# Two full-tile additions of an adaLN block made by accumulating DMAs instead of by GpSimd

## The chip, the cores and the metric

One NeuronCore of a Trainium2 chip runs the whole program, a transformer block over 8 batch rows of 2048 tokens with 256 features, all float32. The metric is the device time of one execution in microseconds (us), lower is better.

## The reference, cut to what matters

```python
h = layernorm(x) * (1 + ca) + sa
a = attention(h)            # per head: softmax over the 64x64 matrix q^T k, then v times it, then w_fc, + b_fc + h
a = layernorm(a) * gamma + beta
x2 = x + ga * a             # = x + (ga*gamma) * norm(..) + ga*beta
h2 = layernorm(x2) * (1 + cb) + sb
y = gb * sigmoid(r(h2)) * (relu(k(h2))**2 @ W_v)    # r and k mix each token with the one before it
out = x2 + y
```

`ga`, `gb`, `ca` and the like are vectors of 256 numbers, one set for each batch row.

## The kernel before, in words

Tokens lie on the 128 partitions. A batch row `b` is cut into four chunks `j` of 512 tokens; a chunk is a tile of 128 partitions by 1024 numbers (four token groups `t` of 256 features), 512 KB. Each engine has its instruction order written out by hand (`row_steps` of each engine), and rows 1 to 5 or 6 run in a hardware loop. The orders interleave three rows: the second half of row `b`, the statistics, transposes and score matrix of row `b+1`, and the loads and statistics of row `b+2`. All joints are semaphores.

The way of one chunk through the second half: TensorE multiplies (`attention`); ScalarE squares (`squares`, L625); GpSimd makes the factor `rs_o` (`rstd_o`, L452 and L454); VectorE scales the product (`make_x2`, L874) and adds `xb` (L881), which gives `x2`; VectorE takes statistics (`stats_2`, L887); GpSimd makes the normalisation factors (`rstd_2`, eleven instructions on 128x4 numbers, L425 to L447); ScalarE normalises (`make_z2`, L679); TensorE transposes; ScalarE copies; VectorE mixes with the token before (`mix`, L901 and L905); then the three products of the second part, with `split_xr` (L642), `low_xr` (L912), `take_r` (L651, writes the gate into `y`), `low_k` (L919) and `gate_o` (L928, makes `y`).

Two additions on whole tiles are GpSimd's: `make_xb` (L462) makes `xb = x_in + ga*beta` for the next row, and `add_y` (L480) makes `y = y + x2`, which SyncE then stores (`store_y`). GpSimd's order in a loop row is `rstd_o(b,0)`, `add_y(b-1,2)`, `rstd_2(b,0)`, `prep_wv` (L469 to L475), `rstd_o(b,1)`, `make_xb(n,0)`, `rstd_2(b,1)`, `make_xb(n,1)`, `rstd_o(b,2)`, `add_y(b-1,3)`, `rstd_2(b,2)`, `make_xb(n,2)`, `rstd_o(b,3)`, `add_y(b,0)`, `make_xb(n,3)`, `rstd_2(b,3)`, two `rstd_a`, `add_y(b,1)`, two `rstd_a`, where `n = b+1`. Before the loop GpSimd makes the four `xb` of row 0. SyncE issues the loads of `x_in` (L294; each waits until `z` and `xb` have been made from the old data), the loads of broadcast rows from a scratch in memory, and the stores. `y` has two buffers by turns; `take_r` waits until the store from its buffer has ended (`y_stored`). In the last row ("alone") the `x_in` buffers serve as more `y` buffers, and `make_x2` waits there until `add_y` of the row before has read the `x2` chunk that it overwrites.

Of the kernel before, what the change touches and what calls it, by code (L numbers as in the profile page):

```python
# [26 lines left out]
ALU = mybir.AluOpType  # L27
# [3 lines left out]
P = 128  # L31


def adaln_block(nc, x, w_qkv, b_qkv, w_fc, b_fc, gamma, beta, w_r, w_k, w_v, mu_r, mu_k, c, wmod, out):
    B, L, D = x.shape
# [6 lines left out]
    CH = L // CT  # L42
    NT = CT // P
# [10 lines left out]
    with ExitStack() as ctx:  # L54
# [9 lines left out]
        def sem(name):  # L64
            return ctx.enter_context(nc.semaphore(name))
# [91 lines left out]
        def y_buf(j, alone):  # L157

            return x_in[:, j] if alone else y[:, j % 2]
# [86 lines left out]
        z_ready = sem("z_ready")  # L246
        z_turned = sem("z_turned")
        z_used = sem("z_used")
        z_t_ready = sem("z_t_ready")
        xb_ready = sem("xb_ready")  # L250
        att_done = sem("att_done")
        ssq_ready = sem("ssq_ready")
        ve_o_done = sem("ve_o_done")
# [21 lines left out]
        th_ready = sem("th_ready")  # L275
        o_done = sem("o_done")
        ro_ready = sem("ro_ready")
        y_ready = sem("y_ready")
        y_end_stored = sem("y_end_stored")
        y_end_ready = sem("y_end_ready")  # L280
        y_stored = [sem(f"y_stored{s}") for s in range(2)]
# [1 line left out]
        def wait_past(eng, semaphore, count):  # L283

            if not isinstance(count, int) or count > 0:
                eng.wait_ge(semaphore, count)
# [4 lines left out]
        @block.sync  # L291
        def _(sp):
            def load_x(b, j):
                sp.dma_start(x_in[:, j], x_v[b, j]).then_inc(x_loaded[j], 16)  # L294

            def load_ca(b):
                src = scratch[b, CA:CA + D].partition_broadcast(P)
                sp.dma_start(rows[:, 3], src).then_inc(ca_loaded, 16)

                sp.dma_start(wqk_aug[P - 1:P, KD - 1, :], scratch[b, QB:QB + QK].unsqueeze(0)).then_inc(edge_loaded, 16)  # L300
                sp.dma_start(res[P - 1:P, KD - 1, :], scratch[b, CB:CB + D].unsqueeze(0)).then_inc(edge_loaded, 16)

            def load_gates(b):

                src = scratch[b, GB:GB + 2 * D].partition_broadcast(P)
                sp.dma_start(rows[:, 0:2].rearrange("p r d -> p (r d)"), src).then_inc(gates_loaded, 16)

            def load_gb(b):
                src = scratch[b, GB + 2 * D:NR].partition_broadcast(P)
                sp.dma_start(rows[:, 2], src).then_inc(gb_loaded, 16)  # L310

            def next_x(b, j):

                sp.wait_ge(z_ready, CH * (b - 1) + j + 1)
                sp.wait_ge(xb_ready, CH * (b - 1) + j + 1)
                load_x(b, j)

            def next_ca(b):

                sp.wait_ge(m_ready, b)  # L320
                sp.wait_ge(wv_ready, b)
                load_ca(b)

            def next_gates(b):

                sp.wait_ge(xb_ready, CH * b)
                sp.wait_ge(now_step, 3 * b - 2)
                load_gates(b)

            def next_gb(b):  # L330

                sp.wait_ge(now_ready, b)
                load_gb(b)

            def store_y(b, j, alone=False):
                sp.wait_ge(y_ready, CH * b + j + 1)
                sp.dma_start(out_v[b, j], y_buf(j, alone)).then_inc(y_stored[j % 2], 16)

            def row_steps(b, first):
                next_gates(b + 1)  # L340
                if not first:
                    store_y(b - 1, 2)
                next_x(b + 2, 0)
                next_x(b + 2, 1)
                if not first:
                    store_y(b - 1, 3)
                next_gb(b + 1)
                next_x(b + 2, 2)
                next_x(b + 2, 3)
                store_y(b, 0)  # L350
                store_y(b, 1)
                next_ca(b + 2)

            wmod_v = wmod.rearrange("(k p) n -> p k n", p=P)
            sp.dma_start(c_sb, c).then_inc(c_loaded, 16)
            load_x(0, 0)
            sp.dma_start(wmod_sb[:, :, 0:2 * D], wmod_v[:, :, 0:2 * D]).then_inc(wmod_a_loaded, 16)
            load_x(0, 1)
            load_x(0, 2)
            sp.dma_start(wmod_sb[:, :, 2 * D:6 * D], wmod_v[:, :, 2 * D:6 * D]).then_inc(wmod_b_loaded, 16)  # L360
            load_x(0, 3)
            for n, w in enumerate((w_r, w_k, w_v)):
                sp.dma_start(w_ffn[:, n], w.rearrange("(k p) n -> p k n", p=P)).then_inc(ffn_loaded, 16)

            sp.wait_ge(row8_a_ready, 1)
            sp.dma_start(scratch[:, 0:GB], row8[:, 0:GB]).then_inc(row8_stored, 16)
            sp.wait_ge(row8_stored, 16)
            load_ca(0)
            sp.wait_ge(row8_b_ready, 1)
            sp.dma_start(scratch[:, GB:NR], row8[:, GB:NR]).then_inc(row8_stored, 16)  # L370
            sp.wait_ge(row8_stored, 32)
            load_gates(0)
            load_gb(0)
            for j in range(CH):
                next_x(1, j)
            next_ca(1)
            row_steps(0, True)
            with sp.Fori(1, B - 2) as b:
                row_steps(b, False)
            next_gates(B - 1)  # L380
            store_y(B - 3, 2)
            store_y(B - 3, 3)
            next_gb(B - 1)
            for b in (B - 2, B - 1):
                for j in range(CH):
                    if b < B - 1 or j < CH - 1:
                        store_y(b, j, alone=(b == B - 1 and j > 0))

            for q in range(2):
                half = slice(2 * q, 2 * q + 2)  # L390
                sp.wait_ge(y_end_ready, q + 1)
                sp.dma_start(out_v[B - 1, CH - 1, :, half], y_buf(CH - 1, True)[:, half]).then_inc(y_end_stored, 16)

            sp.wait_ge(y_stored[0], 16 * B * CH // 2)
            sp.wait_ge(y_stored[1], 16 * (B * CH // 2 - 1))
            sp.wait_ge(y_end_stored, 32)
# [3 lines left out]
        def _(pool):  # L400
# [52 lines left out]
                pool.wait_ge(ve_o_done, i + 1)  # L453
                nc.gpsimd.tensor_tensor(rs_o[:, s], ve_o[:, s], neg_half[:], ALU.pow).then_inc(rs_o_ready, 1)  # L454

            def make_xb(b, j, first=False):
                pool.wait_ge(x_loaded[j], 16 * (b + 1))
                pool.wait_ge(gates_loaded, 16 * (b + 1))
                if not first:

                    pool.wait_ge(x2_ready, CH * (b - 1) + j + 1)
                nc.gpsimd.tensor_tensor(xb[:, j], x_in[:, j], rows[:, 1].unsqueeze(1).to_broadcast([P, NT, D]),  # L462
                                        ALU.add).then_inc(xb_ready, 1)

            def prep_wv(b):

# [8 lines left out]
                nc.gpsimd.tensor_copy(wv_aug[:, :, LAST], vb_col[:, :, b]).then_inc(wv_ready, 1)  # L475

            def add_y(b, j, alone=False):
                i, y_j = CH * b + j, y_buf(j, alone)
                pool.wait_ge(ro_ready, 2 * i + 2)
                nc.gpsimd.tensor_tensor(y_j, y_j, x2[:, j], ALU.add).then_inc(y_ready, 1)  # L480

            def row_steps(b, first, far):

# [58 lines left out]
            pool.wait_ge(vb_ready, 1)  # L542
            prep_wv(0)
            for j in range(CH):
                make_xb(0, j, first=True)
            rstd_a(1, 0)
            rstd_a(1, 1)
            row_steps(0, True, True)
# [7 lines left out]
        def _(act):  # L556
# [56 lines left out]
            def squares(b, j, alone=False):  # L613


                i, s = CH * b + j, j % 2
                if alone:
                    act.wait_ge(xb_ready, i + 1)
                elif j == CH - 1:
                    wait_past(act, y_ready, CH * b)  # L620
                sq_out = x_in if alone else x2
                for t in range(NT):
                    if t % 2 == 0:
                        act.wait_ge(att_done, 2 * i + t // 2 + 1)
                    sq = nc.scalar.activation(sq_out[:, j, t], att_banks(j, alone)[t // 2][:, (t % 2) * D:(t % 2 + 1) * D], ACT.Square,  # L625
                                              scale=float(D) ** -0.5, accum_out=ssq[:, s, t:t + 1])
                sq.then_inc(ssq_ready, 1)
# [150 lines left out]
        def _(dve):  # L778
# [89 lines left out]
            def make_x2(b, j, mixes=None, alone=False):  # L868

                i, s = CH * b + j, j % 2  # L870
                wait_past(dve, xk_mixed, CH * b + (max(j - 1, 0) if mixes is None else mixes))
                dve.wait_ge(rs_o_ready, i + 1)
                for t in range(NT):
                    ins = nc.vector.scalar_tensor_tensor(t_buf[:, t], att_banks(j, alone)[t // 2][:, (t % 2) * D:(t % 2 + 1) * D],  # L874
                                                         rs_o[:, s, t:t + 1], g_row[:], ALU.mult, ALU.mult)
                ins.then_inc(t_done, 1)
                dve.wait_ge(t_done, i + 1)
                dve.wait_ge(xb_ready, i + 1)
                if alone:
                    dve.wait_ge(y_ready, CH * (b - 1) + j + 1)  # L880
                nc.vector.tensor_tensor(x2[:, j], t_buf[:], xb[:, j], ALU.add).then_inc(x2_ready, 1)  # L881

            def stats_2(b, j):
# [595 lines left out]
```

## Time and profile before

| | |
|---|---|
| time, median of 3 runs | 775.9 us (775.25 to 776.17) |
| the profiled execution | 776.98 us; its span 775.2 us |
| mean granted TensorE clock in it | 0.971 |
| stores of `y` / loads of `x_in`, 512 KB each | 31 whole ones and two halves / 32 |
| issue to landing, median | 3.0 us / 3.5 us |
| DMA queues' share of 16 engines | 16.3% (SyncE's queue), 1.0% (ScalarE's) |
| one loop row (GpSimd's L469 at 173.1, 262.1, 352.5, 442.9, 531.8 us) | 89.0 to 90.4 us |

The span runs from the first to the last instruction; the 1.8 us between it and the execution's time lie around the program. A timeline row gives start and duration of an instruction (or of some in a row, x2, x4), and in brackets how long its engine had been idle and what released it. The trace names the `x2` tile `x`.

### The profile page before, as it was taken

The numbers are of one execution on the slowest core, as the hardware profiler recorded it, in microseconds if no ns is written. First come the engines' busy times: TensorE is split into PE (matmuls) and PEld (weight loads), VectorE is DVE, ScalarE is ACT, GpSimd is POOL, SyncE is SP. The second block draws the span as 40 slices with busy tenths as digits, with TensorE's granted clock in tenths as the row PEclk, the third lists the DMA queues.
The fourth block names the chain that finished last, engine by engine and source line by source line (L and its number), as shares of the span: only waits on it lengthen the run. The fifth ranks groups of instructions, "written<-read, shape, count | busy, mean of one in ns | idle before, by whom it ended". The sixth has DMA issues, their size and how long they took to land.

```text
span 775.2 us, 11980 instructions
## 1 busy us (share of the span) xinstructions
PE 679.2 (88%) x3810; PEld 545.9 (70%) x3810; DVE 626.0 (81%) x1063; ACT 422.8 (55%) x903; POOL 497.3 (64%) x809
## 2 busy tenths in 40 slices
PE   5958888998889888998889989898889988898687
PEld 1847776886768775877768867687758777687565
DVE  4595879968998699886999589986998879857864
ACT  0323563565655466455745656554754557456654
POOL 4155897588656785768755886558856687407542
PEclk8989988999999999999999999999999999999999
DMA  9213021111211122010210112120221101100002
GB/s 314 66 52 100 1 89 54 35 42 48 69 55 48 54 61 81 28 48 27 88 54 34 41 54 61 54 70 31 61 81 33 42 0 34 39 16 28 28 27 82
DMA packets 40810, 43.22 MB, mean 56 GB/s; under 512 B 2697, under 2 KB 38833, under 8 KB 40785
## 3 DMA queue, kind: packets, MB, share of 16 engines
q1 hardware_dynamic: 38704, 40.24, 16.3%
q10 hardware_dynamic: 2080, 2.68, 1.0%
q8 instruction: 12, 0.20, 0.1%
q14 instruction: 14, 0.11, 0.0%
HBM read 26.06 MB, written 16.85 MB: 55 GB/s over the span
## 4 chain that ended last, share of the span: by engine, by line
POOL 40%; DVE 19%; issue 18%; PE 17%; DMA 2%; ACT 2%; POOLq 1%; DVEq 0%; ACTq 0%
POOL xb L462 5%; DVE x L881 3%; POOL ag L437 3%; POOL y L480 3%; POOL rs_o L454 3%; POOL ag_a L437 3%; DVE xk L905 3%; DVE t_buf L874 3%; POOL ag L425 2%; POOL ag L431 2%; PE work L1308 2%; POOL wv_aug L469 2%; POOL ag L427 2%; POOL ag_a L431 2%; DVE st L887 2%
## 5 line engine op out<-in xcount | busy, mean ns | idle before, releaser
L1258 PE MATMUL att<-m_sb,z_t 128*128 128x256 f32 x496 | 113.3, 381 | 17.3 <-DVE t_buf L874 16.3
L679 ACT ACTIVATE z<-x,ag 128x256 f32<-128x256 f32 x128 | 66.4, 590 | 100.5 <-POOL ag L447 100.5
L1258 PEld LDWEIGHTS att<-m_sb,z_t 128*128 128x128 f32 x496 | 92.3, 190 | 35.1 <-issue 23.9
L874 DVE SCALAR_TENSOR_TENSOR t_buf<-att,rs_o,g_row 128x256 f32<-128x256 f32 x124 | 51.4, 478 | 68.7 <-POOL rs_o L454 68.6
L1308 PE MATMUL work<-xk,w_k_t 128*128 128x512 f32 x236 | 106.2, 592 | 0.0
L1142 PE MATMUL work<-wvf_lo,k_hi 128*128 128x256 f32 x248 | 75.8, 306 | 28.3 <-issue 23.8
L462 POOL TENSOR_TENSOR xb<-x_in,rows 128x1024 f32<-128x1024 f32 x32 | 79.3, 2482 | 16.0 <-DMA rows<-row_scratch 8.5
L1240 PE MATMUL gram<-z 128*128 128x256 f32 (+1 forms) x512 | 89.1, 327 | 0.0
L425 POOL TENSOR_TENSOR ag<-st 128x4 f32<-128x4 f32 x32 | 20.6, 643 | 102.4 <-DVE st L887 102.4
L1240 PEld LDWEIGHTS gram<-z 128*128 128x128 f32 x512 | 79.8, 191 | 6.6
L1142 PE MATMUL work<-w_r_lo,xr_hi 128*128 128x256 f32 x232 | 69.1, 298 | 11.6 <-DVE xr_lo L912 11.6
L1142 PEld LDWEIGHTS work<-wvf_lo,k_hi 128*128 128x128 f32 x248 | 49.9, 201 | 41.2 <-issue 34.1
L480 POOL TENSOR_TENSOR y<-y,x 128x1024 f32<-128x1024 f32 x29 | 68.8, 2373 | 9.8 <-DVE y L928 9.8
L1308 PEld LDWEIGHTS work<-xk,w_k_t 128*128 128x128 f32 x236 | 42.8, 190 | 42.6 <-issue 42.6
L642 ACT ACTIVATE xr_hi<-xr 128x1024 fp32r<-128x1024 f32 x30 | 31.6, 1054 | 75.3 <-DVE xr L905 75.2
L1144 PE MATMUL work<-wvf_hi,k_lo 128*128 128x256 f32 x248 | 72.7, 293 | 0.0
L1143 PE MATMUL work<-wvf_hi,k_hi 128*128 128x256 f32 x248 | 72.6, 293 | 0.0
L1143 PE MATMUL work<-w_r_hi,xr_hi 128*128 128x256 f32 x232 | 66.3, 286 | 0.0
L1144 PE MATMUL work<-w_r_hi,xr_lo 128*128 128x256 f32 x232 | 66.2, 285 | 0.0
L864 DVE TENSOR_SCALAR z<-x_in,ag_a 128x255 f32<-128x255 f32 x128 | 56.2, 501 | 7.7 <-PE gram L1240 3.9
L625 ACT ACTIVATE x<-att 128x256 f32<-128x256 f32 x116 | 42.9, 379 | 23.9 <-PE att L1258 23.8
L881 DVE TENSOR_TENSOR x<-t_buf,xb 128x1024 f32<-128x1024 f32 x32 | 52.1, 1629 | 4.1 <-POOL y L480 3.0
(187 smaller groups left out, 1780.1 us busy)
## 6 DMA issues: line engine op xcount, KB each, us to landing
x_in<-in_L_attn_x_dram SPq DMA_DIRECT2D x32, 512.0 KB, 3.5
out_dram<-y SPq DMA_DIRECT2D x29, 512.0 KB, 3.0
rows<-row_scratch SPq DMA_DIRECT2D x16, 128.0 KB, 3.5
rows<-row_scratch SPq DMA_DIRECT2D x8, 256.0 KB, 3.2
wqkv_sb<-in_L_attn_w_qkv_dram ACTq DMA_DIRECT2D x1, 1536.0 KB, 10.7
x<-in_L_wmod_dram SPq DMA_DIRECT2D x1, 1024.0 KB, 14.0
out_dram<-x_in SPq DMA_DIRECT2D x2, 512.0 KB, 3.0
x<-in_L_wmod_dram SPq DMA_DIRECT2D x1, 512.0 KB, 4.6
```

Of the source, the lines that this page charges most:

```text
L462: nc.gpsimd.tensor_tensor(xb[:, j], x_in[:, j], rows[:, 1].unsqueeze(1).to_broadcast([P, NT, D]), ALU.add).then_inc(xb_ready, 1)
L480: nc.gpsimd.tensor_tensor(y_j, y_j, x2[:, j], ALU.add).then_inc(y_ready, 1)
L679: ins = nc.scalar.activation(z2[:, t], x2[:, j, t], ACT.Identity, bias=ag_2[:, s, 1, t:t + 1], scale=ag_2[:, s, 7, t:t + 1])
L864: ins = nc.vector.tensor_scalar(z[:, j % 2, t, 0:LAST], x_in[:, j, t, 0:LAST], ag_a[:, j, 3, t:t + 1], ag_a[:, j, 7, t:t + 1], ALU.subtrac ...
L874: ins = nc.vector.scalar_tensor_tensor(t_buf[:, t], att_banks(j, alone)[t // 2][:, (t % 2) * D:(t % 2 + 1) * D], rs_o[:, s, t:t + 1], g_ro ...
L881: nc.vector.tensor_tensor(x2[:, j], t_buf[:], xb[:, j], ALU.add).then_inc(x2_ready, 1)
L1142: mm(dst, s_hi, m_lo, start=start, stop=False)
L1143: mm(dst, s_hi, m_hi, start=False, stop=False)
L1144: return mm(dst, s_lo, m_hi, start=False, stop=stop)
L1240: ins = mm(gram[:, k * D:(k + 1) * D - k * P], z[:, j % 2, t, k * P:(k + 1) * P], z[:, j % 2, t, k * P:D], start=(j == 0 and t == 0 and k ...
L1258: ins = mm(att_banks(j, alone)[q][:, (t % 2) * D:(t % 2 + 1) * D], z_t[:, j, k, t * P:(t + 1) * P], m_sb[:, k], start=(k == 0), stop=(k == ...
L1308: ins = mm(k_banks(alone)[dh][:], w_k_t[:, ch, rows_dh], mixed(j, alone)[1][:, ch], start=(ch == 0), stop=(ch == KD - 1))
```

## The change: what it does

`make_xb` and `add_y` are DMAs issued by GpSimd that add in flight. For `x2 + y`, SyncE stores `x2` to the output as soon as it is made, and GpSimd's DMA adds `y` to it in memory. For `x + ga*beta`, SyncE fills the `xb` chunk with the broadcast row (as soon as `x2` of the old row is made), and GpSimd's DMA adds `x`, read again from memory, to it. The waits follow: the loads of `x_in` and of the gates no longer wait for `xb`; `squares` waits for the store of the old `x2` chunk; `make_x2` waits for the DMA into its `xb` chunk. The order of GpSimd's steps stays as it is; SyncE's order is new.

```diff
             def load_gates(b):
-                src = scratch[b, GB:GB + 2 * D].partition_broadcast(P)
-                sp.dma_start(rows[:, 0:2].rearrange("p r d -> p (r d)"), src).then_inc(gates_loaded, 16)
+                src = scratch[b, GB:GB + D].partition_broadcast(P)
+                sp.dma_start(rows[:, 0], src).then_inc(gates_loaded, 16)
+            def fill_xb(b, j):
+                src = scratch[b, GB + D:GB + 2 * D].partition_broadcast(P).unsqueeze(1).to_broadcast([P, NT, D])
+                sp.dma_start(xb[:, j], src).then_inc(xb_filled[j], 16)
...
-            def store_y(b, j, alone=False):
-                sp.wait_ge(y_ready, CH * b + j + 1)
-                sp.dma_start(out_v[b, j], y_buf(j, alone)).then_inc(y_stored[j % 2], 16)
+            def store_x2(b, j):
+                sp.wait_ge(x2_ready, CH * b + j + 1)
+                sp.dma_start(out_v[b, j], x2[:, j]).then_inc(x2_stored[j], 16)
+            def store_and_fill(b, j):
+                store_x2(b, j)
+                fill_xb(b + 1, j)
+            def row_steps(b):
                 next_gates(b + 1)
                 next_x(b + 2, 0)
                 next_x(b + 2, 1)
+                store_and_fill(b, 0)
+                next_x(b + 2, 2)
+                store_and_fill(b, 1)
                 next_gb(b + 1)
+                store_and_fill(b, 2)
                 next_x(b + 2, 3)
+                store_and_fill(b, 3)
                 next_ca(b + 2)
...
             load_gb(0)
             for j in range(CH):
+                fill_xb(0, j)
+            for j in range(CH):
                 next_x(1, j)
...
+            def make_xb(b, j):
+                pool.wait_ge(xb_filled[j], 16 * (b + 1))
+                nc.gpsimd.dma_start(xb[:, j], x_v[b, j], accum_op=ALU.add).then_inc(xb_ready[j], 16)
...
             def add_y(b, j, alone=False):
                 pool.wait_ge(ro_ready, 2 * i + 2)
-                nc.gpsimd.tensor_tensor(y_j, y_j, x2[:, j], ALU.add).then_inc(y_ready, 1)
+                pool.wait_ge(x2_stored[j], 16 * (b + 1))
+                nc.gpsimd.dma_start(out_v[b, j], y_buf(j, alone), accum_op=ALU.add).then_inc(y_stored[j % 2], 16)
...
-                dve.wait_ge(xb_ready, i + 1)
+                dve.wait_ge(xb_ready[j], 16 * (b + 1))
                 if alone:
-                    dve.wait_ge(y_ready, CH * (b - 1) + j + 1)
+                    dve.wait_ge(x2_stored[j], 16 * b)
```

## Rows read from the trace of the kernel before

**Rows 1.** The page, part 1: busy time of each engine over the span.

```profile
PE 679.2 (88%) x3810; PEld 545.9 (70%) x3810; DVE 626.0 (81%) x1063; ACT 422.8 (55%) x903; POOL 497.3 (64%) x809
```

**Rows 2.** The page, part 4: the chain that ended last, shares by engine.

```profile
POOL 40%; DVE 19%; issue 18%; PE 17%; DMA 2%; ACT 2%; POOLq 1%; DVEq 0%; ACTq 0%
```

**Rows 3.** Busy us by stretch, one loop row: length, engines, TensorE clock, DMA.

```profile
262.00:352.00 90.00, 81.61 (x463) 66.35 (x462) 77.35 (x128) 51.84 (x112) 61.69 (x100) 0.98 0.17 53
```

**Rows 4.** VectorE waiting for others, same row (us in total, times, longest).

```profile
DVE t_buf L874 <- POOL rs_o L454: 10.0, 3, 6.3
```

**Rows 5.** Groups of instructions, GpSimd (busy us, mean ns, idle before).

```profile
L462 POOL TENSOR_TENSOR xb<-x_in,rows 128x1024 f32<-128x1024 f32 x32 | 79.3, 2482 | 16.0 <-DMA rows<-row_scratch 8.5 <-DVE x L881 7.5
L480 POOL TENSOR_TENSOR y<-y,x 128x1024 f32<-128x1024 f32 x29 | 68.8, 2373 | 9.8 <-DVE y L928 9.8
```

**Rows 6.** Timeline of GpSimd in that row: start, duration, instruction, idle before.

```profile
277.72 2.37 POOL L462 TENSOR_TENSOR xb<-x_in,rows 128x1024 f32<-128x1024 f32 x1
291.05 2.88 POOL L462 TENSOR_TENSOR xb<-x_in,rows 128x1024 f32<-128x1024 f32 x1
294.62 1.40 POOL L454 TENSOR_TENSOR rs_o<-ve_o,neg_half 128x4 f32<-128x4 f32 x1
297.65 2.39 POOL L480 TENSOR_TENSOR y<-y,x 128x1024 f32<-128x1024 f32 x1 [1.63 <-DVE y L928]
301.30 2.35 POOL L462 TENSOR_TENSOR xb<-x_in,rows 128x1024 f32<-128x1024 f32 x1 [1.25 <-DVE x L881]
310.10 0.21 POOL L425 TENSOR_TENSOR ag<-st 128x4 f32<-128x4 f32 x1 [6.45 <-DVE st L887]
```

**Rows 7.** Timeline of VectorE in that row.

```profile
277.74 2.89 DVE L953 TENSOR_TENSOR wvf_lo<-t_buf,wvf_hi 128x512 fp32r<-128x512 f32 x1
281.82 1.66 DVE L874 SCALAR_TENSOR_TENSOR t_buf<-att,rs_o,g_row 128x256 f32<-128x256 f32 x4 [1.19 <-POOL rs_o L454]
297.49 1.66 DVE L874 SCALAR_TENSOR_TENSOR t_buf<-att,rs_o,g_row 128x256 f32<-128x256 f32 x4
299.18 1.95 DVE L881 TENSOR_TENSOR x<-t_buf,xb 128x1024 f32<-128x1024 f32 x1
301.35 3.38 DVE L901 TENSOR_TENSOR t_buf<-h2t 128x1024 f32<-128x1024 f32 x1 [0.22 <-PE work L1308]
```

**Rows 8.** By source line, ns min/median/max, then first and last start.

```profile
L881 DVE TENSOR_TENSOR x<-t_buf,xb x32: 1224/1678/1961, 73.9 to 731.0; 128x1024 f32<-128x1024 f32 x32
...
L901 DVE TENSOR_TENSOR t_buf<-h2t x32: 1206/1216/3383, 86.7 to 750.9; 128x1024 f32<-128x1024 f32 x32
...
L431 POOL TENSOR_SCALAR ag<-ag x32: 192/193/1728, 77.6 to 740.0; 128x4 f32<-128x4 f32 x32
```

**Rows 9.** Timeline of ScalarE in that row.

```profile
294.07 1.05 ACT L642 ACTIVATE xr_hi<-xr 128x1024 fp32r<-128x1024 f32 x1
317.37 1.31 ACT L651 ACTIVATE y<-work 128x512 f32<-128x512 f32 x2
```

**Rows 10.** Timeline of TensorE around 309 us.

```profile
308.81 0.36 PE L1142 MATMUL work<-wvf_lo,k_hi 128*128 128x256 f32 x1 [2.40 <-issue]
310.97 0.41 PE L1142 MATMUL work<-wvf_lo,k_hi 128*128 128x256 f32 x1
```

**Rows 11.** By tile, x_in: SyncE's issues (ns), and issue to landing (us).

```profile
L294 SPq DMA_DIRECT2D x_in<-in_L_attn_x_dram x32: 368/373/518, 1.2 to 573.6; - x32
DMA to landing us min/median/max: 2.6/3.5/15.1
```

**Rows 12.** Timeline of SyncE at the start, its slowest issue.

```profile
5.45 5.75 SPq L363 DMA_DIRECT2D y<-in_L_ffn_W_k_dram  x1
```

**Rows 13.** Timeline of VectorE: start, first row, last row.

```profile
52.13 4.76 DVE L1002 TENSOR_TENSOR attn<-s_exp,s_inv 64x256 f32<-64x256 f32 x2
121.11 5.63 DVE L905 SCALAR_TENSOR_TENSOR xr<-t_buf,mu_col,h2t 128x512 f32<-128x512 f32 x2
...
730.99 1.23 DVE L881 TENSOR_TENSOR x<-t_buf,xb 128x1024 f32<-128x1024 f32 x1 [3.00 <-POOL y L480]
```

More of the change, by code:

```diff
@@ L249, in adaln_block @@
         z_t_ready = sem("z_t_ready")
-        xb_ready = sem("xb_ready")
+        xb_filled = [sem(f"xb_filled{j}") for j in range(CH)]
+        xb_ready = [sem(f"xb_ready{j}") for j in range(CH)]
         att_done = sem("att_done")
@@ L277, in adaln_block @@
         ro_ready = sem("ro_ready")
-        y_ready = sem("y_ready")
+        x2_stored = [sem(f"x2_stored{j}") for j in range(CH)]
         y_end_stored = sem("y_end_stored")
@@ L314, in next_x @@
                 sp.wait_ge(z_ready, CH * (b - 1) + j + 1)
-                sp.wait_ge(xb_ready, CH * (b - 1) + j + 1)
                 load_x(b, j)
@@ L324, in next_gates @@
             def next_gates(b):
-                sp.wait_ge(xb_ready, CH * b)
                 sp.wait_ge(now_step, 3 * b - 2)
@@ L333, in next_gb @@
                 load_gb(b)
-            def store_y(b, j, alone=False):
-                sp.wait_ge(y_ready, CH * b + j + 1)
-                sp.dma_start(out_v[b, j], y_buf(j, alone)).then_inc(y_stored[j % 2], 16)
-            def row_steps(b, first):
+            def store_x2(b, j):
[5 more added lines that the diff above has]
+            def row_steps(b):
                 next_gates(b + 1)
-                if not first:
-                    store_y(b - 1, 2)
                 next_x(b + 2, 0)
                 next_x(b + 2, 1)
-                if not first:
-                    store_y(b - 1, 3)
+                store_and_fill(b, 0)
+                next_x(b + 2, 2)
+                store_and_fill(b, 1)
                 next_gb(b + 1)
-                next_x(b + 2, 2)
+                store_and_fill(b, 2)
                 next_x(b + 2, 3)
-                store_y(b, 0)
-                store_y(b, 1)
+                store_and_fill(b, 3)
                 next_ca(b + 2)
@@ L374, in _ @@
             for j in range(CH):
+                fill_xb(0, j)
+            for j in range(CH):
                 next_x(1, j)
             next_ca(1)
-            row_steps(0, True)
+            row_steps(0)
             with sp.Fori(1, B - 2) as b:
-                row_steps(b, False)
+                row_steps(b)
             next_gates(B - 1)
-            store_y(B - 3, 2)
-            store_y(B - 3, 3)
+            store_and_fill(B - 2, 0)
+            store_and_fill(B - 2, 1)
             next_gb(B - 1)
[L384 to L387, printed above, removed]
+            store_and_fill(B - 2, 2)
+            store_and_fill(B - 2, 3)
+            for j in range(CH - 1):
+                store_x2(B - 1, j)
             for q in range(2):
@@ L454, in rstd_o @@
                 nc.gpsimd.tensor_tensor(rs_o[:, s], ve_o[:, s], neg_half[:], ALU.pow).then_inc(rs_o_ready, 1)
[L456 to L463, printed above, removed]
+            def make_xb(b, j):
+                pool.wait_ge(xb_filled[j], 16 * (b + 1))
+                nc.gpsimd.dma_start(xb[:, j], x_v[b, j], accum_op=ALU.add).then_inc(xb_ready[j], 16)
             def prep_wv(b):
@@ L477, in add_y @@
             def add_y(b, j, alone=False):
-                i, y_j = CH * b + j, y_buf(j, alone)
+                i = CH * b + j
                 pool.wait_ge(ro_ready, 2 * i + 2)
-                nc.gpsimd.tensor_tensor(y_j, y_j, x2[:, j], ALU.add).then_inc(y_ready, 1)
+                pool.wait_ge(x2_stored[j], 16 * (b + 1))
+                nc.gpsimd.dma_start(out_v[b, j], y_buf(j, alone), accum_op=ALU.add).then_inc(y_stored[j % 2], 16)
             def row_steps(b, first, far):
@@ L544, in _ @@
             for j in range(CH):
-                make_xb(0, j, first=True)
+                make_xb(0, j)
             rstd_a(1, 0)
@@ L617, in squares @@
                 if alone:
-                    act.wait_ge(xb_ready, i + 1)
-                elif j == CH - 1:
-                    wait_past(act, y_ready, CH * b)
+                    act.wait_ge(z_ready, i + 1)
+                else:
+                    wait_past(act, x2_stored[j], 16 * b)
                 sq_out = x_in if alone else x2
```

## The prediction, made before the changed kernel ran

> **What bounds the kernel now.** The page's busy shares come first [rows 1]: TensorE 88%, VectorE 81%, GpSimd 64%. No engine is full, so a wait or the order of work sets the pace. The chain that ended last says which [rows 2]: GpSimd holds 40% of it, VectorE 19%, TensorE 17%. The engine with a middling busy share is on the path most. Next one loop row by itself [rows 3]: of 90.0 us TensorE is busy 81.6, VectorE 77.4, GpSimd 61.7, the DMA engines 0.17. The first number is the floor: a row cannot fall much below 81 us whatever GpSimd does, so at most some 8.4 us a row are to be had. The waits of the same row [rows 4]: VectorE stands 10.0 us in three places, each time for `rs_o`, the small factor that GpSimd makes. GpSimd's groups [rows 5] give the two additions that leave it: 32 of 2.48 us and 29 of 2.37 us (and two in the last row).
>
> The timelines show two ways in which a whole-tile addition hurts. First by order: in the second chunk GpSimd ends its normalisation factors at 277.7, then spends 2.37 us on `xb`, and only then makes the `rs_o` for which VectorE is idle 1.19 us [rows 6, 7]. Second by slowing VectorE: while such an addition runs, VectorE's own additions of two tiles take longer. L881 takes 1.22 us at best, 1.68 at the median, 1.96 at most; L901 1.21 at the median and 3.38 at 301.35, exactly beside the `xb` of 301.30 [rows 6 to 8].
>
> **The change, part by part, for one loop row.** The new quantity is T, the time for which GpSimd is held by issuing one adding DMA; the trace has none. From below stands SyncE's issue of a plain 512 KB DMA, 0.37 us [rows 11]; from above SyncE's slowest issue, 5.75 us [rows 12], and a tile pass of GpSimd is 2.37 to 2.48 us [rows 5]. I take T = 2.0: nearer to the tile pass than to the issue of SyncE, since 512 pieces of 1 KB have to be described for two sides. Then eight times a row 2.4 us become 2.0, which is little; the gain lies in where the rest goes.
>
> 1. *The addition `x2` no longer meets a GpSimd pass.* Chunks 0, 1 and 2 go from the median 1.68 to 1.22, the fourth from 1.95 to 1.22 [rows 7, 8]: 3 x 0.45 + 0.7 = 2.05 us. All four stand before the statistics that GpSimd waits for, so they count in full.
> 2. *`rs_o` of the third chunk comes earlier by 2.37 - T = 0.4 us.* VectorE could use it: the 2.89 us of L953 from 277.74 [rows 7] were themselves stretched by the `xb` beside them, and become less than the 4.1 us until L874.
> 3. *L901 of the third mix, 3.38 to 1.21: 2.2 us.* VectorE has no gap from 297.49 to there [rows 7], and what comes behind it is `low_k` and the statistics of the fourth chunk.
> 4. *TensorE's gap before `ffn_out`, 2.40 us, closes*, because it waits for that `low_k` [rows 10]. Behind the gap the matmuls slow down: one at 310.97 takes 0.41 us, the first took 0.36 [rows 10]. Over the whole row the granted clock is 0.98, which on 81.6 busy us is some 1.6 us [rows 3]. The gap itself closes by items 1 to 3 and is not counted again; of the 1.6 I take 1.0 (bounds 0 and 1.6).
> 5. *The stretched second mix (L905) is worth nothing.* It lies beside ScalarE's copy of `xr`, which begins at 294.07 [rows 9] and on which the next VectorE step waits; that copy hangs on GpSimd's factors. The cover is about 2 us.
> 6. *What the new waits cost.* The fill of chunk j starts when `x2` of that chunk is made and SyncE has issued the store: 2 x 0.37 us, then 3.5 us as a load of the same size [rows 11], and 1.4 us more since the store goes ahead of it on the same queue (my estimate, some 40% of a landing). So a fill is there 5.6 us after `x2`. GpSimd stands at `make_xb` until then, with all that is queued behind it. For chunk 0 the DMA is due 12 us later or more. For chunk 2, `x2` is ready about 285 and the `xb` step is at 291.05: just enough. `rs_o` behind it ends at 296.0 and is used at 297.49 [rows 6, 7], so T may grow to 2.88 + 1.5 = 4.4 us there. For chunk 3 it is late: in the clock of the old trace `x2` ends at 300.4, the fill lands at 306.0, GpSimd is free at 308.0, and the statistics it should take up are ready at 310.1 [rows 6] less 0.7 and 2.2, that is 307.2. Cost 0.8 us, of which I count 0.6 because the exponentials behind it have a little slack.
> 7. *Landing of the adding DMAs.* `xb` for chunk 3 has most of a row until its use. `y` of chunk 0 is issued at 297.65 and its buffer is written again at 317.37 [rows 6, 9]: 19.7 us of cover for something whose plain relatives take 3.5 at the median and 15.1 at most [rows 11]. Nothing counted. The DMA share rises from 0.17 [rows 3]: two transfers of 512 KB a chunk become five, with two of them reading twice, so about 0.17 x 7 / 2 = 0.6. That fits.
>
> SyncE's moved steps: `next_x` loses its wait for `xb` and comes earlier; the stores of `x2` wait for VectorE only, and no step behind them is due before. `next_gates` and `next_gb` keep waits that end early in the row. Nothing counted.
>
> Sum: 2.05 + 0.4 + 2.2 + 1.0 - 0.6 = 5.05 us a row. With six such rows (1 to 6) 30 us. TensorE's floor allows it: 5.05 of 8.4.
>
> *Row 0*: the pair of L905 at 121.11 takes 5.63 where two plain ones take 1.5 [rows 13]: 4 us. *Last row*: VectorE's wait of 3.00 us for `add_y` turns into a wait for a store long ended [rows 13]: 3 us. *Start*: the addition beside `attn` made that 4.76 instead of about 0.85 us [rows 13], a gain of 3.9. Against it four fills go ahead of the loads of row 1 on SyncE's queue, up to 4 x 3.5 = 14 us if they don't overlap, and the statistics of those loads stand in VectorE's order before the matrix that starts row 0. I set the two equal: 0, bounds +4 and -10. *End*: the last whole chunk went 2.37 + 3.0 us by addition and store, now T + 3.5 to 7 us by one DMA: 1 us lost (0 to 4).
>
> Total 30 + 4 + 3 + 0 - 1 = 36. The profiled execution is 776.98 us, so 741; it stands 1.1 us above the median of 775.9, so I predict **740 us**. With T = 0.4 item 2 gives 1.6 more and item 6 falls away, 2.2 a row: about 727. With T = 4, the row keeps 5.05 - 2 x 2.0 = 1.05 (each us of T counts in items 2 and 6): 764.
>
> L881 and L901 are slowed beside a tile pass of GpSimd [rows 6 to 8]. The Trainium skill (SBUF — State Buffer, section "Who interferes with whom") says that a VectorE instruction with two inputs in SBUF contends with a GpSimd instruction that reads SBUF, and the page infers that building descriptors needs the write side, which such an instruction leaves free. The trace agrees with the first half; no row here shows the second. By it T stays at its undisturbed value and items 1 and 3 come in full. The same page, section "SBUF: two separate sides", speaks against the change: a DMA of GpSimd has its descriptors written by software, and one that takes 0.62 us alone took 3.1 us beside a VectorE copy. An estimate by that 3.1: 5.05 - 2.2 = 2.85 us a row, 754 us in all; rival A works out the same kind of hindrance from rows.
>
> **Rivals.**
>
> *A, GpSimd's issue and VectorE still hinder each other (0.15).* For it: a 128x4 step of GpSimd takes 0.19 us and up to 1.73 [rows 8] when VectorE is in the way, so each issue may be held 1.5 us, T = 3.5. Against: GpSimd no longer streams tiles. The row keeps 5.05 - 3.0 = 2.05; 6 x 2.05 + 4 + 3 - 1 = 18, so 759 us.
>
> *B, slower: the issue of an adding DMA holds GpSimd longer than the addition did (0.20).* Each stands in GpSimd's order before small factors that the other engines wait for. Items 2 and 6 lose T - 2 each; zero is reached at T = 2 + 5.05 / 2 = 4.5 us. At the upper bound 5.75 they cost 7.5, and the `rs_o` of chunk 3 (allowed 4.4) another 1.35: 3.8 us lost a row, 27 over seven, and the last row's 3 back, 4 lost at the end: 805 us. For it: one plain issue did take 5.75 [rows 12]. Against: the 32 loads of `x_in` took 0.37 to 0.52 to issue [rows 11].
>
> *C, slower: the fill lands late (0.07).* GpSimd stands at `make_xb` and all factors behind it wait. At the 15.1 us that one load took [rows 11], `make_xb` of chunk 2 ends about 303 and its `rs_o` 304.9, 7.4 us after VectorE wants it; with the gains left some 7 to 8 us are lost a row, 830 us. Against: that load was one of the start's crowd.
>
> *D, a tie (0.06)*: T near 4.5, or adding DMAs that land after the 19.7 us of item 7, give back just the gain: 776 us. That the additions don't leave GpSimd at all is excluded, since they are no longer its instructions.
>
> **How the numbers follow.** The forecast, with its own range 720 to 768, has 0.52. A and the forecast are faster: 0.67. The tie, and measurements of this kernel can't tell 0.2% (1.6 us) from no change, has 0.06. B and C are slower: 0.27. The range 718 to 800 leaves out the upper part of B, C, and a little below.
>
> **What would show it.** GpSimd's busy time should fall by the 148 us of [rows 5] (issuing a DMA isn't counted as busy), L881 be near 1.22 us in all chunks, L901 never above 1.3, VectorE's wait for `rs_o` below 10 us a row, a row about 85 us. SyncE's and GpSimd's waits tell item 6: a wait of GpSimd for the fills above 2 us a row means C; small factors that follow an issue by more than 3 us mean B. Most likely to be wrong is T, then the start.

## The result, and the profile after

The changed kernel takes **819.5 us** at the median (814.4 to 823.5, 4 runs), beside 775.6 us for the kernel before on the same chip: ratio 1.058 [1.050, 1.065]. It is slower, outside the range; the prediction said 740 us. The execution shown here took 817.35 us, its span is 815.8 us.

The page of the changed kernel, parts 1, 3 and 4, and one group of part 5 (busy us and mean ns; idle time before it, and what ended it):

```profile
span 815.8 us, 12092 instructions
...
PE 688.3 (84%) x3810; PEld 549.3 (67%) x3810; DVE 556.4 (68%) x1063; ACT 421.0 (52%) x903; POOL 407.5 (50%) x809
...
q1 hardware_dynamic: 55600, 55.97, 28.4%
q0 software_dynamic: 33264, 33.03, 27.3%
...
DMA 31%; POOL 25%; issue 15%; DVE 13%; PE 10%; ACT 2%; SPq 2%; POOLq 1%; DVEq 0%; ACTq 0%
...
L466 POOL DMA_DIRECT2D xb<-in_L_attn_x_dram x32 | 42.6, 1331 | 165.5 <-DMA xb<-row_scratch 165.5
```

Against [rows 1], VectorE has 70 us and GpSimd 90 us less to do: both reliefs came. Yet every engine is idle longer. The chain says why: DMA holds 31% of it and held 2% before [rows 2]. The last line names the transfer. GpSimd stands 165.5 us at the adding DMA of `make_xb` (L466), waiting for the fill of `xb` from `row_scratch`.

Part 6 of the page: KB of each DMA, median us from issue to landing.

```profile
x_in<-in_L_attn_x_dram SPq DMA_DIRECT2D x32, 512.0 KB, 5.9
xb<-row_scratch SPq DMA_DIRECT2D x32, 512.0 KB, 9.9
xb<-in_L_attn_x_dram POOLq DMA_DIRECT2D x32, 512.0 KB, 5.9
out_dram<-x SPq DMA_DIRECT2D x31, 512.0 KB, 4.4
out_dram<-y POOLq DMA_DIRECT2D x29, 512.0 KB, 6.1
```

The adding DMAs land in 5.9 and 6.1 us. The slow one is the plain fill: 9.9 us, where the prediction worked with 3.5 for the same bytes, and 1.4 more for the store ahead.

The chain of waits, one loop row (start us, us, what). It answers to [rows 2] at the scale of a row:

```profile
288.91 1.02 POOL rs_o L461
...
290.35 1.27 DVE t_buf L878 x3
291.65 1.24 DVE x L885
293.17 0.40 SPq L340
293.67 9.70 DMA xb<-row_scratch
...
304.04 1.34 POOL xb L466
305.38 0.24 POOL ve_o L459
305.71 1.03 POOL rs_o L461
...
307.17 1.27 DVE t_buf L878 x3
308.46 1.24 DVE x L885
309.85 0.40 SPq L340
310.33 10.12 DMA xb<-row_scratch
```

It is a loop through four parties: `rs_o` lets VectorE make `x2` of a chunk, SyncE stores it and fills `xb` of that chunk, the fill lets GpSimd issue `make_xb`, and behind that in GpSimd's order stands the `rs_o` of the next chunk. One turn is 16.8 us, 10 of them the fill. GpSimd's timeline shows the same from its side (start, duration, idle before); it answers to [rows 6]:

```profile
304.03 1.35 POOL L466 DMA_DIRECT2D xb<-in_L_attn_x_dram  x1 [2.38 <-DMA xb<-row_scratch]
305.70 1.03 POOL L461 TENSOR_TENSOR rs_o<-ve_o,neg_half 128x4 f32<-128x4 f32 x1
306.70 1.32 POOL L484 DMA_DIRECT2D out_dram<-y  x1
...
321.08 1.34 POOL L466 DMA_DIRECT2D xb<-in_L_attn_x_dram  x1 [5.50 <-DMA xb<-row_scratch]
322.74 1.03 POOL L461 TENSOR_TENSOR rs_o<-ve_o,neg_half 128x4 f32<-128x4 f32 x1
...
338.54 1.28 POOL L466 DMA_DIRECT2D xb<-in_L_attn_x_dram  x1 [13.49 <-DMA xb<-row_scratch]
339.32 0.74 POOL L432 TENSOR_TENSOR ag<-st 128x4 f32<-128x4 f32 x1
```

Three chunks wait for their fills, 21.4 us in this row. The issue itself holds GpSimd for 1.3 us.

*Where the 40.6 us of span come from.* The starts of `prep_wv` (L469 before, L472 after) mark the rows, the first `x2` the end of the start. (The five times that the table of the kernel before gives for L469 are those of its L472, 2.5 us later; the row lengths there hold.)

| stretch (us) | before | after | difference |
|---|---|---|---|
| span's start to first `x2` addition | 73.85 | 98.33 | +24.5 |
| to `prep_wv` of the first loop row | 96.8 | 91.6 | -5.1 |
| five loop rows | 449.1 | 467.7 | +18.6 |
| from there to the end | 155.5 | 158.1 | +2.6 |

A row is 93.5 us instead of 89.8. So there are two losses, the start and the row, and both were to be explained. VectorE's timeline at the start, answering to [rows 13]:

```profile
51.23 0.85 DVE L1006 TENSOR_TENSOR attn<-s_exp,s_inv 64x256 f32<-64x256 f32 x2
...
81.50 1.40 DVE L858 BATCH_NORM_STATS2 st_a<-x_in 128x6 f32<-128x256 f32 x4 [28.70 <-DMA x_in<-in_L_attn_x_dram]
```

`attn` is short, as forecast, but the statistics behind it wait 28.7 us for the loads that stand behind four fills on SyncE's queue. What TensorE and the DMA engines do meanwhile (columns as in [rows 3], the last two DMA share and GB/s):

```profile
60.00:66.00 6.00, 0.29 (x2) 0.00 (x0) 0.00 (x0) 0.00 (x0) 1.30 (x1) 0.70 0.87 83
```

The DMA engines are 87% busy and move only 83 GB/s. GpSimd's issues of `make_xb` follow the fills at 56.8, 63.6, 70.0 and 77.4 us: 6.4 to 7.4 us for each fill of 512 KB. Little else moves meanwhile, though it has been issued: the adding DMA of 56.8 lands 24.3 us later.

### The profile page after: what moved, and what is told of

It reads as the page before. It is cut to its first block, busy times and chain, and to the rows that moved or that the text cites. A ratio compares the mean times of both kernels' runs of the same rounds, so it can differ in the third digit from the quotient of the medians.

```text
span 815.8 us, 12092 instructions
## 1 busy us (share of the span) xinstructions
PE 688.3 (84%) x3810; PEld 549.3 (67%) x3810; DVE 556.4 (68%) x1063; ACT 421.0 (52%) x903; POOL 407.5 (50%) x809
## 4 chain that ended last, share of the span: by engine, by line
DMA 31%; POOL 25%; issue 15%; DVE 13%; PE 10%; ACT 2%; SPq 2%; POOLq 1%; DVEq 0%; ACTq 0%
DMA xb<-row_scratch 26%; DVE t_buf L878 4%; DMA x_in<-in_L_attn_x_dram 4%; DVE x L885 4%; POOL rs_o L461 3%; POOL xb L466 2%; POOL ag L444 2%; PE att L1262 2%; POOL ag L432 2%; PE work L1312 1%; POOL out_dram L484 1%; POOL ag_a L438 1%; POOL wv_aug L472 1%; DMA wqkv_sb<-in_L_attn_w_qkv_dram 1%; POOL wv_aug L475 1%
## 5 line engine op out<-in xcount | busy, mean ns | idle before, releaser
L1262 PE MATMUL att<-m_sb,z_t 128*128 128x256 f32 x496 | 115.7, 387 | 47.7 <-DVE m_sb L1013 27.9
L1262 PEld LDWEIGHTS att<-m_sb,z_t 128*128 128x128 f32 x496 | 94.0, 193 | 66.3 <-issue 54.3
L1312 PE MATMUL work<-xk,w_k_t 128*128 128x512 f32 x236 | 115.9, 631 | 22.1 <-ACT y L655 22.1
L466 POOL DMA_DIRECT2D xb<-in_L_attn_x_dram x32 | 42.6, 1331 | 165.5 <-DMA xb<-row_scratch 165.5
L1148 PE MATMUL work<-wvf_hi,k_lo 128*128 128x256 f32 x248 | 71.0, 286 | 0.0
L1147 PE MATMUL work<-wvf_hi,k_hi 128*128 128x256 f32 x248 | 70.9, 286 | 0.0
L858 DVE BATCH_NORM_STATS2 st_a<-x_in 128x6 f32<-128x256 f32 x128 | 44.5, 409 | 34.5 <-DMA x_in<-in_L_attn_x_dram 34.3
L432 POOL TENSOR_TENSOR ag<-st 128x4 f32<-128x4 f32 x32 | 23.2, 725 | 71.1 <-DVE st L891 71.1
L1146 PEld LDWEIGHTS work<-w_r_lo,xr_hi 128*128 128x128 f32 x232 | 44.4, 191 | 11.6 <-DVE xr_lo L916 11.6
L868 DVE TENSOR_SCALAR z<-x_in,ag_a 128x255 f32<-128x255 f32 x128 | 45.8, 419 | 9.4 <-POOL ag_a L444 5.3
```

The lines of the kernel that those rows point to most:

```text
L466: nc.gpsimd.dma_start(xb[:, j], x_v[b, j], accum_op=ALU.add).then_inc(xb_ready[j], 16)
L858: ins = nc.vector.bn_stats(st_a[:, j, t], x_in[:, j, t])
L868: ins = nc.vector.tensor_scalar(z[:, j % 2, t, 0:LAST], x_in[:, j, t, 0:LAST], ag_a[:, j, 3, t:t + 1], ag_a[:, j, 7, t:t + 1], ALU.subtrac ...
L1146: mm(dst, s_hi, m_lo, start=start, stop=False)
L1147: mm(dst, s_hi, m_hi, start=False, stop=False)
L1148: return mm(dst, s_lo, m_hi, start=False, stop=stop)
```

## The experiments

Each was timed in three rounds beside the kernel before (775.85 us in the first four, 775.32 in the rest). The ratio is to that kernel. Diffs are against the changed kernel unless said, and show the main lines; `...` marks what is left out. The length of a row is the mean of the five loop rows of the profiled execution.

Theory one, *the source of the fill*: all 512 pieces of a fill read the same 1 KB row, and that makes it slow. Theory two, *the traffic*: five transfers a chunk share the DMA engines, and a fill is slow because much is in flight or the store is ahead of it. Theory three, *GpSimd and VectorE still hinder each other* (rival A), or the issue is long (B).

**e1: the same pieces, another source.**

```diff
-                src = scratch[b, GB + D:GB + 2 * D].partition_broadcast(P).unsqueeze(1).to_broadcast([P, NT, D])
-                sp.dma_start(xb[:, j], src).then_inc(xb_filled[j], 16)
+                sp.dma_start(xb[:, j], x_v[b, j]).then_inc(xb_filled[j], 16)
```

> The kernel after, but the fill of xb reads 512 different rows of x (the chunk itself) instead of one row of ga*beta 512 times; so xb is 2x, not x + ga*beta. Same 512 KB, same 1 KB pieces, same order and waits. Theory S (one source row read by every piece is slow): a fill lands in 4.5 to 6 us instead of 9.9, GpSimd's wait for fills falls from 165 to under 40 us, the start loses some 5 us instead of 24, and the time is 735 to 765 us. Rival Q (the DMA queues are too full, or 1 KB pieces beside adding DMAs are slow): a fill still lands in 9 to 10 us and the time stays 810 to 825.

Measured: 736.1 us, ratio 0.950 [0.947, 0.954]. Its page, part 6:

```profile
xb<-in_L_attn_x_dram SPq DMA_DIRECT2D x32, 512.0 KB, 6.0
xb<-in_L_attn_x_dram POOLq DMA_DIRECT2D x32, 512.0 KB, 6.1
```

Number, size and target of the pieces, their place in the queue and all traffic are as in the changed kernel; only the addresses read differ. The fill lands in 6.0 us instead of 9.9, a row takes 84.1 us, and 83 us are gone. Theory two cannot say this. One expectation was missed: GpSimd still waits 82.8 us in all for fills (165.5 before the edit), where under 40 were expected. In a loop row it waits 10.4 to 10.8 us, and the row is no longer than in e5 and e8 below, where it waits for no fill: there is slack for this much.

**e2: only the half of `y`**, against the kernel before: `xb` stays an addition of GpSimd.

```diff
+            def store_x2(b, j):
+                sp.wait_ge(x2_ready, CH * b + j + 1)
+                sp.dma_start(out_v[b, j], x2[:, j]).then_inc(x2_stored[j], 16)
...
-                nc.gpsimd.tensor_tensor(y_j, y_j, x2[:, j], ALU.add).then_inc(y_ready, 1)
+                pool.wait_ge(x2_stored[j], 16 * (b + 1))
+                nc.gpsimd.dma_start(out_v[b, j], y_buf(j, alone), accum_op=ALU.add).then_inc(y_stored[j % 2], 16)
...
```

> Only the half that concerns y: x2 is stored, y is added in memory by GpSimd's DMA; xb is made on GpSimd as before, with no fills. Theory W (all that was lost was lost waiting for fills): this half is a gain by itself, since GpSimd is held 1.33 us instead of 2.4 and VectorE is slowed less: 755 to 765 us. Rival (adding DMAs into memory cost time of their own, at the end or by their traffic): 776 or more.

Measured: 760.6 us, 0.981 [0.976, 0.985]; a row 87.2 us. This half gains 15 us; the changed kernel, which has the `xb` half on top, is 59 us slower than this one. So the loss comes with `xb`. VectorE is busy 603.7 us, between 626.0 and 556.4: each half takes away part of the slowing. Part 3 of the page (packets, MB, share of the 16 DMA engines' time) prices the adding DMAs, which alone are on q0 here:

```profile
q1 hardware_dynamic: 38704, 40.24, 16.3%
q0 software_dynamic: 16368, 16.25, 15.6%
```

They keep the DMA engines busy 2.4 times as long for a byte as the plain ones do (0.96% for a MB against 0.41).

**e3: the fill ahead of the store.**

```diff
-                store_x2(b, j)
+                sp.wait_ge(x2_ready, CH * b + j + 1)
                 fill_xb(b + 1, j)
+                store_x2(b, j)
```

> The kernel after, with the fill issued ahead of the store of x2 on SyncE instead of behind it. At the start, with no store ahead, four fills took about 6.6 us each. Theory S with queueing behind the store as the second part: a fill lands in about 7 us instead of 9.9, GpSimd waits some 50 to 70 us less in all and the time falls to 795 to 805 us; the start keeps its 24 us. If the store had no part in it: 9 to 10 us and 815 to 820.

Measured: 788.9 us, 1.018 [1.014, 1.021]; a row 88.5 us. Part 6 of its page:

```profile
xb<-row_scratch SPq DMA_DIRECT2D x32, 512.0 KB, 8.9
xb<-in_L_attn_x_dram POOLq DMA_DIRECT2D x32, 512.0 KB, 6.0
out_dram<-x SPq DMA_DIRECT2D x31, 512.0 KB, 9.7
```

The landing was expected at 7 us and is 8.9: the store costs the fill 1.0 us, less than the 1.4 of the prediction, and the fill is slow even when it is first. The store now pays for standing behind it, 9.7 instead of 4.4 us. The time fell by 31 us, more than the 1.0 us of median landing explains at sight; one turn of the loop above also loses the store's issue (0.4 us), and the wait of GpSimd fell by 27 us. The expected 795 to 805 us was missed, on the fast side; how much each gives was not taken apart.

**e4: the row is loaded once, the fill copies it from on-chip memory.**

```diff
-                src = scratch[b, GB:GB + D].partition_broadcast(P)
-                sp.dma_start(rows[:, 0], src).then_inc(gates_loaded, 16)
+                src = scratch[b, GB:GB + 2 * D].partition_broadcast(P)
+                sp.dma_start(rows[:, 0:2].rearrange("p r d -> p (r d)"), src).then_inc(gates_loaded, 16)
...
-                src = scratch[b, GB + D:GB + 2 * D].partition_broadcast(P).unsqueeze(1).to_broadcast([P, NT, D])
+                sp.wait_ge(gates_loaded, 16 * (b + 1))
+                src = rows[:, 1].unsqueeze(1).to_broadcast([P, NT, D])
...
             def next_gates(b):
+                for j in range(CH):
+                    sp.wait_ge(xb_filled[j], 16 * b)
```

> The kernel after, but the row of ga*beta is loaded once per batch row into the rows tile (128 KB, as before the change) and the fill copies it from there inside on-chip memory, each partition its own row. Nothing is left out. Theory S: no row in memory is read by all pieces, so a fill lands in 4 to 6 us and the time is 735 to 765 us. Rival Q: 9 to 10 us, 810 to 825 us.

Measured: 743.6 us, 0.959 [0.955, 0.963]; the full computation. Part 6:

```profile
xb<-rows SPq DMA_DIRECT2D x32, 512.0 KB, 5.9
```

Each piece now reads the copy of its own partition (four pieces share it), and the fill lands in 5.9 us. A row takes 84.1 us, as in e1. The 7.5 us above e1 lie in the start: the first `x2` comes at 83.8 instead of 75.6 us. Waiting for the load of the row explains part of it: the four fills are issued 2.8 us later than in e1 (51.04 instead of 48.27). The first statistics of row 1's load then begin 7.6 us later (67.74 instead of 60.16); where the rest comes from was not found.

**e5: the same slow fills, but `make_xb` later in GpSimd's order.**

```diff
                     rstd_o(b, 1)
-                    make_xb(n, 0)
                     rstd_2(b, 1)
-                    make_xb(n, 1)
                     rstd_o(b, 2)
                     add_y(b - 1, 3)
+                    make_xb(n, 0)
                 rstd_2(b, 2)
...
-                make_xb(n, 2)
                 rstd_o(b, 3)
...
+                make_xb(n, 1)
                 add_y(b, 0)
-                make_xb(n, 3)
                 rstd_2(b, 3)
...
                 add_y(b, 1)
+                make_xb(n, 2)
...
+                make_xb(n, 3)
```

> The kernel after with the fill as it is (slow, one row of memory), but GpSimd issues the adding DMAs of xb later in its order, where the fills have long landed: chunk 0 behind add_y(b-1,3), chunk 1 behind rstd_o(b,3), chunk 2 behind add_y(b,1), chunk 3 at the row's end. Theory: it is GpSimd standing in a wait, with the small factors behind it, that costs the rows, not the traffic; then the waits for fills in the loop vanish, only the start's (some 31 us on GpSimd, 24 us in the time) stay, and the time is 755 to 770 us. Rival: slow fills and adding DMAs disturb the rows by traffic: 800 or more.

Measured: 759.2 us, 0.979 [0.977, 0.981]. Part 6 of its page, then GpSimd's and VectorE's waits over the whole span (us in total, times, longest):

```profile
xb<-row_scratch SPq DMA_DIRECT2D x32, 512.0 KB, 11.3
```

```profile
POOL xb L466 <- DMA xb<-row_scratch: 32.2, 4, 14.9
```

```profile
DVE st_a L856 <- DMA x_in<-in_L_attn_x_dram: 35.7, 4, 30.1
```

This is the run that tells the wait from the transfer. The fills are slower than ever, 11.3 us, and the rows don't mind: 84.2 us each, as with fast fills. The four waits that are left are those of the start. A slow transfer cost a row something only while an engine with work for others stood in front of it.

**e6: the start as before**: `xb` of row 0 is made by GpSimd's additions, no fills go ahead of the first loads.

```diff
-                fill_xb(0, j)
+                sp.wait_ge(xb0_ready, j + 1)
...
-                make_xb(0, j)
+                pool.wait_ge(x_loaded[j], 16)
+                pool.wait_ge(gates_loaded, 16)
+                nc.gpsimd.tensor_tensor(xb[:, j], x_in[:, j], rows[:, 1].unsqueeze(1).to_broadcast([P, NT, D]),
+                                        ALU.add).then_inc(xb0_ready, 1)
...
```

> The kernel after, but xb of row 0 is made by GpSimd as before the change, so no fills go ahead of the loads of row 1. Theory: the start's loss is those four fills, 24 us; time 791 to 799 us. Rival: the start's loss is hidden later or comes from elsewhere: above 805.

Measured: 794.5 us, 1.025 [1.022, 1.027]: 25.0 us less than the changed kernel, where the table above has 24.5 for the start. The first `x2` is at 72.95 us and a row still 93.6. The two losses are separate and add up.

**e7: the row four times in memory**, so that a fill is 128 pieces of 4 KB.

```diff
-                src = scratch[b, GB + D:GB + 2 * D].partition_broadcast(P).unsqueeze(1).to_broadcast([P, NT, D])
+                src = wide[b, 0:NT * D].partition_broadcast(P)
...
+            for t in range(NT):
+                sp.dma_start(wide[:, t * D:(t + 1) * D], row8[:, GB + D:GB + 2 * D]).then_inc(wide_stored, 16)
```

> The kernel after, but the row of ga*beta stands four times in a row in memory and the fill reads these 4 KB by each of 128 partitions: 128 pieces of 4 KB instead of 512 of 1 KB, each byte read 128 times instead of 512. Theory S in its form 'a rate per place read': a fill gets near the pace of other 512 KB transfers (5 to 7 us) and the time is 740 to 760. If any row read by all partitions is slow at the same bytes a second: 9 to 10 us and 815 to 825.

Measured: 743.1 us, 0.958 [0.956, 0.960]. Part 6, then a stretch of the start as in the window above:

```profile
xb<-wide_scratch SPq DMA_DIRECT2D x32, 512.0 KB, 6.3
```

```profile
54.00:60.00 6.00, 5.22 (x13) 3.70 (x12) 0.00 (x0) 1.19 (x2) 3.57 (x3) 0.51 0.72 262
```

262 GB/s where the changed kernel moves 74 in the same six microseconds. Each byte is still read 128 times by a fill, so it isn't sharing as such that is slow, nor the scratch memory, but 512 small pieces from one 1 KB row. The run doesn't tell whether fewer pieces or four times as many source bytes did it.

**e8: e4, e5 and e6 together**, the full computation.

> The fill on chip of e4, the later issue of e5 and the start of e6 together; nothing is left out. Theory: no wait for fills is left, GpSimd is held 1.33 us by an issue and VectorE is not slowed: 718 to 732 us. Rival: TensorE's busy 81 us a row is reached before: 735 to 744, no better than e4.

Measured: **733.3 us**, 0.945 [0.943, 0.947], the fastest of all. Its waits hold no fill any more. One row (columns as in [rows 3]):

```profile
246.80:331.00 84.20, 80.83 (x467) 66.97 (x466) 67.64 (x128) 52.16 (x112) 52.76 (x100) 0.98 0.60 131
```

It came out 1 us above its range, 10 us below e4: the start gave 9.0 us (first `x2` at 74.8), the rows nothing more. TensorE has work for 80.8 of the row's 84.2 us. The trace names what it waits for in the rest (us in total, times, longest):

```profile
PE work L1154 <- DVE k_lo L931: 2.3, 1, 2.3
PE work L1154 <- DVE xr_lo L924: 0.8, 2, 0.5
PE att L1270 <- DVE t_buf L883: 0.3, 1, 0.3
```

In the row of [rows 3] the same view adds up to 8.3 us.

## Why the prediction was wrong, step by step

**The step that failed is item 6**, "a fill is there 5.6 us after `x2`", and with it the start's "up to 4 x 3.5 = 14 us". Both took the fill for "a load of the same size", 3.5 us. It lands 9.9 us after its issue, of which the store ahead is only 1.0 (e3), and four of them in a row take 6.4 to 7.4 us each. The reason (e1, e4, e7) is one whose sign stands in the diff and that the prediction passed over: the source is a broadcast of one row in both directions, `partition_broadcast` and `to_broadcast`, 512 pieces of 1 KB from the same 1 KB. The page of the kernel before had a nearer relative than [rows 11], one that the prediction did not use. Part 6, the broadcast load of two rows to all partitions:

```profile
rows<-row_scratch SPq DMA_DIRECT2D x8, 256.0 KB, 3.2
```

Half the bytes in nearly the time of a whole-tile load (3.5 us) was a warning, no more: doubled, it gives 6.4 us, which is also what a fill takes at the start, but these are 128 pieces from one row, of the kind that e7 shows to be fast. With 6.4 us in place of 3.5, item 6 would have read 8.5 us after `x2`, and chunk 2 would no longer have been "just enough".

**The mechanism in the rows was rival C's**, told rightly: GpSimd stands at `make_xb` and the factors behind it are late. Its sign, a wait for fills above 2 us a row, came with 21.4 us, but alone it proves little: in e1 the wait is 10.6 us and costs nothing. VectorE's wait for `rs_o` tells more: 10.0 us in the row before [rows 4], 14.8 to 16.1 in the changed kernel's loop rows, 11.1 in e1. C's price was off. Its 830 us lie all in the rows, 7 to 8 us lost in each; a row lost 3.7, and more than half of the loss, 24.5 us, is the start's, which C doesn't have. That 830 is near 819.5 is luck. Its chance of 0.07 was too small, for a reason that was on the page: item 6 had found the fill of chunk 2 "just enough" and that of chunk 3 late at 5.6 us, so anything slower had to stop GpSimd ahead of `rs_o`. A step without slack whose duration is an estimate deserves more than that.

**The start** was set to 0 with bounds +4 and -10. It lost 24.5 us (e6: 25.0). The short `attn` came, 0.85 us, and gave nothing: the work behind it waits for the loads of row 1, which stand behind the fills. Four fills were to take 14 us at most; from the first issue at 47.85 to the last `make_xb` behind them at 77.42 they took 29.6.

**T, said to be the most likely to be wrong**, was 1.33 us, no instance over 1.52:

```profile
L466 POOL DMA_DIRECT2D xb<-in_L_attn_x_dram x32: 1282/1332/1522, 56.8 to 709.8; - x32
```

It was taken as 2.0, so B fell. In e8 it rises, to 1.66 at the median and 2.38 at most, and the trace shows where:

```profile
265.98 1.37 POOL L488 DMA_DIRECT2D out_dram<-y  x1
266.86 1.84 POOL L470 DMA_DIRECT2D xb<-in_L_attn_x_dram  x1
```

Every issue of 1.80 us and more in e8 begins within 0.9 us of another one's start; one that stands by itself takes 1.28 to 1.51 there too.

**Items 1 and 3** came in full, as far as the lengths of the two additions go. By source line (ns min/median/max), answering to [rows 8]:

```profile
L885 DVE TENSOR_TENSOR x<-t_buf,xb x32: 1224/1224/1617, 98.3 to 767.7; 128x1024 f32<-128x1024 f32 x32
```

```profile
L905 DVE TENSOR_TENSOR t_buf<-h2t x32: 1205/1216/2597, 111.2 to 790.8; 128x1024 f32<-128x1024 f32 x32
```

The median of the first was 1678, the worst of the second 3383. One of each is still stretched, 1.62 us at 139.73 and 2.60 at 141.58, both in row 0 and both beside the tile passes that stayed with GpSimd (`prep_wv`, L472 at 137.91 and L475 at 140.34). The eight issues a row do neither side harm, so rival A fell as well: the issue at 304.03, with VectorE idle, takes 1.35 us, and the one at 130.07, in row 0, 1.32, though VectorE's mixing (L909, two inputs from on-chip memory) runs beside it all the time and keeps its usual 1.41 us a pair. The Trainium skill (SBUF — State Buffer, section "Who interferes with whom") infers that writing descriptors doesn't meet a two-input VectorE instruction; the 1.32 us beside L909 agree with that. Its section "SBUF: two separate sides" gives 3.1 us for a GpSimd DMA beside a VectorE copy, which the prediction put in for T; no issue in the changed kernel came near it, and the one at 768.91, beside which VectorE also does a cast of 0.43 us, took 1.33.

**The sum of the row** was right once the fill is out of the way: 5.05 us forecast, 5.6 to 5.7 measured (89.8 down to 84.1 in e1 and e4, 84.2 in e5 and e8), so a row of 85 was 84.2. That e1, which leaves `ga*beta` out of the fill, takes 736 us beside the 740 forecast says the same of the whole: what went wrong was one transfer. The shares of the single items were not measured one by one, so the agreement of the sums may be partly luck. Item 4's gap of 2.40 us is gone in e8, and another of 2.3 has come up before the row's last `ffn_out` (329.51); its 1.0 us for the clock is not shown, the granted clock is 0.98 or 0.99 in e8's rows and was 0.98 to 1.00 before. And one sign didn't come: VectorE's wait for `rs_o` was to fall below 10 us a row and is 11.0 to 11.3 in e1 and e8.

**Item 7** held: the adding DMAs land in 6 us at the median, those of the output in 10.6 at most, under 19.7 us of cover. Those into `xb` take up to 24.3 us, at the start, where nothing waited for them. The DMA share of a row is 0.60 in e8 as forecast. **GpSimd's busy time** fell by 90 us, not by 148: the page does count the issue of its DMAs, 42.6 us for `make_xb` and 38.7 for `add_y` (29 of 1333 ns), which the prediction had said it would not. That leaves some 67 us; the other 20 or so were not taken apart. **Row 0**: the pair that took 5.63 us takes 1.42 (L909 at 144.21), as forecast; the whole stretch is 5.1 us shorter, with other parts in it. The 3.00 us before the last row's `x2` are gone. *The side sums*: 759 (A), 805 (B) and 754 (by the 3.1 us) start from the profiled 776.98 and not, as the forecast does, from the median, so each is 1 us too high; nothing hangs on it.

*What stays open:* what in the memory or the engines holds 512 reads of one row at 80 GB/s; which of e7's two differences cures it; what makes e4's start 8 us longer than e1's; and whether VectorE's late `k_lo`, two thirds of TensorE's idle time in e8's row, could come sooner.

## What to carry to other kernels

Before pricing a DMA by another of the same size, read how many pieces it has and how many of them come from the same bytes: here a 1 KB row read by 512 pieces was cured by four copies in memory, and as well by a copy from a tile on the chip. A DMA whose input is another DMA, issued from an engine that works in order, belongs at a place in that order where the input has long landed; moving it (e5) was worth 60 us while the transfer itself stayed slow. And when one step has no slack and an estimated duration, weigh the case behind it by that, not by how odd it looks.

## What the runs showed that was not expected

- 512 pieces of 1 KB that read one row land in 9.9 us (71 to 82 GB/s alone, by the 7.4 and 6.4 us); as many that read different rows in 6.0; 128 pieces of 4 KB in 6.3; the same 512 from on-chip memory in 5.9.
- A DMA that adds lands in 5.9 to 6.1 us for 512 KB, with 1.33 us of issue on GpSimd; in e2, where the fewest transfers share the engines, 5.9 beside 4.3 for a store and 3.8 for a load. It takes the DMA engines 2.4 times as long for a byte (e2).
- Adding DMAs that are in flight together land later. In e8, with fast fills, those into `xb` take 8.3 us at the median: in a loop row three of four are issued within 3 us of another adding DMA and take mostly 8.0 to 9.6, the one that is not takes 5.9 to 6.1. In e5, with the same order and slow fills, that one takes 9.8 to 11.3, and the median is 9.4. Other transfers overlap them too, so the shares were not separated.
- One slow source slows its neighbours: with it ahead of them in the queue the loads of `x_in` take 5.9 us instead of 5.0 (e1), and the stores 9.7 instead of 4.4 (e3).
